# Two attentions and mixtures of experts: new instruction orders in both attentions, blocks without GpSimd's descriptor drain

## What is computed

```python
x = x + L0_xattn(_layernorm(x), ctx_1024, ctx_1024, fside, fside, pad, mask, ...)   # 16 heads of 16
x = x + L0_ffn(_layernorm(x), ...)      # 14 experts, top 2, 256 -> 512 -> 256
x = x + L1_xattn(_layernorm(x), ctx_1024, ctx_1024, mask, ...)
x = x + L1_ffn(_layernorm(x), ...)      # a shared expert, 8 experts, top 2, 256 -> 1024 -> 256
```

```python
q = (query @ Wq.T + bq).reshape(B, T, H, D).transpose(0, 2, 1, 3)
...
probs = jax.nn.softmax(scores, axis=-1)
out = jnp.einsum('bhts,bhsd->bhtd', probs, v)
```

## Time and profile before

| | us |
|---|---|
| median of 3 runs | 1040.72 (1039.98 to 1042.22) |
| profiled execution: time | 1038.13 |
| its span | 1036.3 |
| mean granted TensorE clock | 0.963 |
| PE busy | 936.5 (90%) |
| DVE, ACT, POOL busy | 498.2, 504.5, 411.6 |

### The profile page before, as it was taken

How to read it: one execution, slowest core, us unless ns; L and a number is a source line. 1 busy time by engine, 2 the same in 40 slices (tenths; PEclk the granted TensorE clock), 3 DMA queues, 4 the chain that set the end, 5 groups by cost and what they waited for, 6 DMA issues and landing times. The chain is left out here.

```text
span 1036.3 us, 25281 instructions
## 1 busy us (share of the span) xinstructions
PE 936.5 (90%) x7420; PEld 826.3 (80%) x7421; DVE 498.2 (48%) x2085; ACT 504.5 (49%) x1434; POOL 411.6 (40%) x534
## 2 busy tenths in 40 slices
PE   2799999788999999649999889998999999999992
PEld 2677787577899999536777679998999999999992
DVE  3587777564333343249999662222232323232315
ACT  2577777423333333238989743343343434343442
POOL 2777767200455555244555250000323333232213
PEclk9899999989899999859999989999999999999996
DMA  5966564077122222135221079200111111101107
GB/s 180 278 189 193 166 194 144 22 264 275 55 68 71 71 71 71 41 103 157 78 80 48 31 244 378 75 11 11 36 35 35 36 35 35 35 35 35 35 17 248
DMA packets 101321, 108.53 MB, mean 105 GB/s; under 512 B 9064, under 2 KB 87546, under 8 KB 100986
## 3 DMA queue, kind: packets, MB, share of 16 engines
q1 hardware_dynamic: 92272, 85.15, 25.6%
q0 software_dynamic: 8064, 22.03, 6.6%
q10 hardware_dynamic: 906, 0.37, 0.2%
HBM read 86.02 MB, written 21.50 MB: 104 GB/s over the span
## 5 line engine op out<-in xcount | busy, mean ns | idle before, releaser
L1846 PEld LDWEIGHTS experts_bank<-xT,wp 128*128 128x128 f32 x1968 | 234.8, 194 | 8.4 <-issue 4.4
L1846 PE MATMUL experts_bank<-xT,wp 128*128 128x128 f32 x1968 | 235.6, 277 | 3.7 <-DVE wp L1926 3.7
L1897 ACT ACTIVATE Hn<-experts_bank,vecT 128x128 f32<-128x128 f32 x312 | 114.3, 367 | 166.2 <-PE experts_bank L1846 147.4
L1778 POOL DMA_INDIRECT token_outputs<-yb,dst x84 | 94.7, 1127 | 215.6 <-DVE yb L1938 215.6
L1457 POOL DMA_INDIRECT rows<-token_rows,src x84 | 90.2, 1074 | 218.9 <-DVE dst L1452 119.6
L1856 PE MATMUL experts_bank<-w,Hn 128*128 x624 | 142.8, 382 | 0.0
L1938 DVE TENSOR_TENSOR yb<-experts_bank,b 128x256 f32<-128x256 f32 x84 | 35.7, 425 | 210.9 <-PE experts_bank L1856 210.9
L1926 DVE COPY wp<-w 128x1024 f32 x123 | 87.8, 714 | 94.7 <-PE experts_bank L1846 93.8
L1856 PEld LDWEIGHTS experts_bank<-w,Hn 128*128 128x128 f32 x624 | 115.4, 190 | 16.0
L1897 ACT ACTIVATE hid<-experts_bank,vecT 128x128 f32<-128x128 f32 x180 | 65.3, 367 | 103.1 <-PE experts_bank L1856 71.4
L1856 PE MATMUL experts_bank<-w,hid 128*128 x360 | 85.0, 379 | 0.0
(11 more groups left out here) (266 smaller groups left out, 1481.5 us busy)
## 6 DMA issues: line engine op xcount, KB each, us to landing
fs<-in_fside_Bx16xSxS_dram SPq DMA_DIRECT2D x32, 512.0 KB, 4.2
w<-in_L_ffn_w_dram SPq DMA_DIRECT2D x28, 512.0 KB
w<-in_L_ffn_Wfc_dram SPq DMA_DIRECT2D x8, 1024.0 KB, 13.8
w<-in_L_ffn_Wproj_dram SPq DMA_DIRECT2D x8, 1024.0 KB, 12.6
ctx<-in_ctx_dram SPq DMA_DIRECT2D x32, 128.0 KB, 4.8
token_rows<-Hn SPq DMA_DIRECT2D x32, 128.0 KB, 3.0
keys_values<-WT SPq DMA_DIRECT2D x16, 256.0 KB, 3.7
y<-token_outputs SPq DMA_DIRECT2D x16, 256.0 KB, 3.1
```

The lines of the kernel that those rows point to most:

```text
L1778: pool.indirect_dma_start(out=c["yg"], out_offset=bass.IndirectOffsetOnAxis(ap=routing["dst"][:, n:n + 1].bitcast(U32), axis=0), in_=yb[n ...
L1846: last = pe.matmul(HB[f % 4][:, 0:P], piece[:, i, (f % CF) * P:(f % CF + 1) * P], xT[par][:, i], start=(i == 0), stop=(i == DC - 1))
L1897: act.activation(hid[par][:, f], HB[f % 4][:, 0:P], moe.act, bias=bias).then_inc(hid_ready, 1)
```

## The change

Three edits. First, in all seven phases `nc.Block()` becomes `nc.Block(no_gpsimd_drain=True)`. In the instruction streams POOL's DRAIN ahead of the first barrier of each block's end is gone; the drains of the other engines, the DRAIN of L67 that comes with the clearing of semaphores, and that of L69 stay. Second, the order in which attention 0's engines call their functions: on PE the groups of outputs stand in two pairs instead of four single groups, project_v goes right behind project_k, and bring comes ahead of turn_e(b-1, 2); ACT has h_out ahead of q_out; DVE has stats ahead of k_out and one group of minima later; POOL has layer_norm of an element one iteration earlier and at the end. Third, the order in attention 1: on PE all four groups of outputs stand together; exps, h_out, minima, residual, et_out and stats move on ACT and DVE; POOL's layer_norm and DVE's stats take element b-1 where they took b-2, and residual and stats stand in one iteration. SP's programs are not touched. The waits of the functions stay, but for two that go from the second group of outputs to the first, since that comes first now. Of the seven hunks of the first edit one stands below.

```diff
--- before.py
+++ after.py
@@ -328,7 +328,7 @@
         ve_ready, rs_ready, nm_ready, h_ready = sem("ve_ready"), sem("rs_ready"), sem("nm_ready"), sem("h_ready")
         hT_done, hT_ready = sem("hT_done"), sem("hT_ready")
         lg_done, lg_ready = sem("lg_done"), sem("lg_ready")
-        block = stack.enter_context(nc.Block())
+        block = stack.enter_context(nc.Block(no_gpsimd_drain=True))
 
         def has(t):
             return 0 <= t < B
@@ -400,15 +400,16 @@
             normed(2)
             pool.wait_ge(amb_ready, 1)
             for b in range(-1, B + 3):
+                if has(b + 1):
+                    add_bo(b + 1)
                 if has(b):
                     bias(b, 1)
-                if has(b - 3):
-                    layer_norm(b - 3)
                 if b >= 0 and has(b + 3):
                     normed(b + 3)
                 if has(b + 1):
                     bias(b + 1, 0)
-                    add_bo(b + 1)
+                if has(b - 2):
+                    layer_norm(b - 2)
 
         @block.tensor
         def _(pe):
@@ -481,7 +482,7 @@
                 last.then_inc(et_done[g], 1)
 
             def outputs(b, g):
-                if g == 1:
+                if g == 0:
                     pe.wait_ge(v_ready, b + 1)
                     if b >= 1:
                         pe.wait_ge(on_ready, b)
@@ -537,34 +538,32 @@
             for b in range(-1, B + 3):
                 if has(b):
                     scores(b)
-                if has(b - 1):
-                    turn_e(b - 1, 2)
                 if has(b + 1):
                     bring(b + 1)
                 if has(b - 1):
-                    outputs(b - 1, 1)
+                    turn_e(b - 1, 2)
                 if has(b - 2):
                     turn_out(b - 2)
                 if has(b - 1):
                     outputs(b - 1, 0)
+                    outputs(b - 1, 1)
                     turn_e(b - 1, 3)
-                    outputs(b - 1, 2)
+                if has(b - 2):
+                    project_out(b - 2)
                 if has(b + 1):
                     project_q(b + 1)
-                if has(b - 2):
-                    project_out(b - 2)
+                if has(b - 1):
+                    outputs(b - 1, 2)
+                    outputs(b - 1, 3)
                 if has(b):
                     turn_e(b, 0)
-                if has(b - 1):
-                    outputs(b - 1, 3)
                 if has(b - 3):
                     turn_h(b - 3)
                 if has(b + 1):
                     project_k(b + 1)
+                    project_v(b + 1)
                 if has(b):
                     turn_e(b, 1)
-                if has(b + 1):
-                    project_v(b + 1)
                 if has(b - 1):
                     turn_back(b - 1)
                 if has(b - 3):
@@ -612,6 +611,7 @@
 
             for b in range(-1, B + 3):
                 if has(b - 1):
+                    exps(b - 1, 3)
                     et_out(b - 1, 2)
                 if has(b + 1):
                     in_out(b + 1)
@@ -619,14 +619,13 @@
                     exps(b, 0)
                     exps(b, 1)
                     et_out(b, 0)
+                if has(b - 3):
+                    h_out(b - 3)
                 if has(b + 1):
                     q_out(b + 1)
-                if has(b - 3):
-                    h_out(b - 3)
                 if has(b):
                     exps(b, 2)
                     et_out(b, 1)
-                    exps(b, 3)
 
         @block.vector
         def _(dve):
@@ -717,16 +716,14 @@
             mask()
             dve.wait_ge(vones_ready, 2)
             for b in range(-1, B + 3):
-                if has(b):
-                    minima(b, 3)
                 if has(b - 2):
                     residual(b - 2)
                 if has(b - 1):
                     o_out(b - 1)
+                if has(b - 2):
+                    stats(b - 2)
                 if has(b + 1):
                     k_out(b + 1)
-                if has(b - 2):
-                    stats(b - 2)
                 if has(b - 1):
                     divide(b - 1)
                 if has(b - 3):
@@ -734,13 +731,15 @@
                 if has(b + 1):
                     v_out(b + 1)
                     minima(b + 1, 0)
-                    minima(b + 1, 1)
                 if has(b - 1):
                     turned(b - 1)
+                if has(b + 1):
+                    minima(b + 1, 1)
                 if has(b):
                     et_out(b)
                 if has(b + 1):
                     minima(b + 1, 2)
+                    minima(b + 1, 3)
 
 
 def attention1(nc, sem, alloc, a, c, routing, shared, moe):
@@ -886,13 +885,13 @@
                 pool.memset(kside[i][:], 0.0).then_inc(kzero_ready, 1)
             for i in two:
                 pool.memset(vaug[i][:], 1.0).then_inc(vones_ready, 1)
-            for b in range(-3, B + 2):
-                if has(b - 2):
-                    layer_norm(b - 2)
+            for b in range(-3, B + 1):
                 if has(b + 2):
                     normed(b + 2)
                 if has(b + 3):
                     add_moe(b + 3)
+                if has(b - 1):
+                    layer_norm(b - 1)
                 if has(b + 1):
                     v_in(b + 1)
 
@@ -998,25 +997,23 @@
                     scores(b)
                 if has(b - 2):
                     turn_out(b - 2)
+                if has(b - 3):
+                    turn_h(b - 3)
                 if has(b - 1):
                     turn_e(b - 1, 2)
-                    outputs(b - 1, 1)
-                    outputs(b - 1, 0)
-                if has(b - 3):
-                    turn_h(b - 3)
                 if has(b - 2):
                     project_out(b - 2)
+                if has(b - 1):
+                    turn_e(b - 1, 3)
                 if has(b + 1):
                     bring(b + 1)
                 if has(b - 1):
-                    turn_e(b - 1, 3)
-                    outputs(b - 1, 2)
+                    for g in groups:
+                        outputs(b - 1, g)
+                if has(b):
+                    turn_e(b, 0)
                 if has(b - 3):
                     logits(b - 3)
-                if has(b - 1):
-                    outputs(b - 1, 3)
-                if has(b):
-                    turn_e(b, 0)
                 if has(b + 1):
                     project_q(b + 1)
                 if has(b):
@@ -1070,7 +1067,6 @@
 
             for b in range(-1, B + 3):
                 if has(b - 1):
-                    exps(b - 1, 1)
                     et_out(b - 1, 0)
                     exps(b - 1, 2)
                 if has(b):
@@ -1080,12 +1076,13 @@
                     exps(b - 1, 3)
                 if has(b - 2):
                     turned(b - 2)
+                if has(b - 3):
+                    h_out(b - 3)
                 if has(b - 1):
                     et_out(b - 1, 2)
-                if has(b - 3):
-                    h_out(b - 3)
                 if has(b):
                     exps(b, 0)
+                    exps(b, 1)
                 if has(b + 1):
                     in_out(b + 1)
 
@@ -1160,17 +1157,13 @@
 
             for b in range(-3, B + 3):
                 if has(b - 1):
-                    et_out(b - 1)
-                if has(b + 3):
-                    combine(b + 3)
-                if has(b - 2):
-                    stats(b - 2)
-                if has(b - 1):
                     o_out(b - 1)
                 if has(b - 3):
                     logits_out(b - 3)
                 if has(b):
                     minima(b, 3)
+                if has(b + 3):
+                    combine(b + 3)
                 if has(b - 1):
                     divide(b - 1)
                 if has(b + 2):
@@ -1178,9 +1171,14 @@
                 if has(b + 1):
                     minima(b + 1, 0)
                     minima(b + 1, 1)
-                    minima(b + 1, 2)
                 if has(b - 1):
                     residual(b - 1)
+                if has(b):
+                    et_out(b)
+                if has(b - 1):
+                    stats(b - 1)
+                if has(b + 1):
+                    minima(b + 1, 2)
 
 
 def at(b):
...
```

## The result

The changed kernel takes 1014.25 us (median of 4 runs, 1013.62 to 1015.99) against 1040.35 (4 runs, 1039.82 to 1042.22): a ratio of 0.9749, 95% interval 0.9731 to 0.9766, 26.1 us less. Forecast were 1015.5, so 25.3 less than the median before the change. The profiled execution took 1014.64, with a span of 1012.9.

A forecast was written before the change was run, and what follows sets the result against it. PE was taken to bound attention 0, three engines nearly level in attention 1, and POOL's drain to idle all engines after experts0. -7.8 - 7.2 - 7.2 - 3.1 = -25.3 from 1040.7 gives 1015.5 us, range 1011.5 to 1030.5.

The forecast's parts named there:

- The sum over islands: Attention 0 on PE: fewer separate runs of narrow output matmuls save 0.61 us an element, giving 9.62; whole term -7.8 us.
- the fourth turn_e: Attention 0 on PE: tightest operand, needing ACT's ET copy of the third; about even, charged 0.04 us an element.
- Attention 1: One run of output matmuls brings PE from 8.10 to about 7.5 us; DVE then sets the period, 7.85; -7.2 us.
- DVE with the least idle time: Sign for attention 1: DVE idles least, with scores 7.8 to 7.9 us apart and no wait for qT.
- tight place: Attention 1: xn for bring(b+1), made by POOL from DVE's statistics, is asked for earlier by PE, with all outputs queued behind.
- The drain: End of layer 0's experts: without POOL's drain the 7.25 us with every engine idle goes; -7.2 us.
- rival A: Blocks' ends: the drain's work moves to L67's DRAIN, which would take 4 to 7 us; 1029.0 us, chance 0.20.
- A2: Blocks' ends: the idle 7.2 us would hit any next POOL instruction, and the end gains nothing; 1025.7 us, chance 0.06.
- POOL's first work within 1.5 us: Sign behind layer 0's last scatter: POOL works again within 1.5 us, with no stretch of all engines idle.
- The end: Kernel's end: without POOL's drain only what lies after SP's own drain is saved, 3.0 us, with semaphore hops -3.1.
- Rival C: Attentions: waits replace the savings, attention 1 stays at 8.37 us, attention 0 gets half; 1026.5 us, chance 0.04.
- Rival D: Attention 1: PE idles more and TensorE's clock falls, +5.6 us an element, 1106 us with all 16; chance 0.03.

The follow-up runs named there:

- e6: Changed kernel with attention 0's two pairs of output groups split again into four single groups on PE, other orders kept; 1022.4 us.
- e2: Kernel before with only the change's attention 0, all engines' orders, and every block with its drain; 1030.87 us.
- e9: Changed kernel with the second of DVE's two combine operations in attention 1 done by POOL as a product and a sum; 1011.9 us.
- e8b: Changed kernel with attention 1's outputs in two pairs on PE, one ahead of bring and one behind, project_out and turn_e left in place; 1011.46 us.
- e8: Changed kernel with attention 1's outputs in two pairs on PE, the first moved ahead of project_out; 1024.0 us.
- e5: Kernel before with every second scatter of layer 0's experts issued twice, the second after the first has landed; 1075.97 us in one run.
- e4: Changed kernel with POOL's drain left out only at the end of layer 0's experts and back in the six other blocks; 1015.49 us.
- e1: Kernel before with no_gpsimd_drain=True in all seven blocks and nothing else changed; 1030.32 us.

## Why the prediction was right

*The number.* 1015.5 were forecast and 1014.25 measured, and part of this nearness is luck. In the two traces the change takes off 23.4 us, 1.9 less than the sum: the end gave 2.2 less than forecast and setup took 1.1 more, and the other phases gave 1.3 more. From median to median it is 26.1, 0.8 more than the sum. The 2.7 us between the two come from where the profiled executions lie among the runs of their kernels. Three mechanisms of four held in size; the fourth held too, but something else took most of it away.

*Attention 0.* The sum over islands holds: 9.62 by the rows, 9.63 measured, 0.59 less an element where 0.57 was charged; of the waits there is one, 0.05 at the fourth turn_e, where the prediction had it. e6 shows the cause. The phase gained 8.4 in the trace of the change and 7.7 in e2.

*Attention 1.* Forecast 7.85 with DVE as the bound, measured 7.78 with DVE 98% busy; the records of DVE overlap a little (those of L1113 are 0.29 long and stand 0.21 apart), which the prediction had as its upper bound (7.75). The phase gained 7.5 (forecast 7.2). The mechanism is the forecast one: PE comes down until DVE sets the period. PE's share was overpriced, though: its stream without waits is 7.60 (e9), 0.50 below 8.10 where 0.59 was charged, so PE had 0.19 to spare. The sign "DVE with the least idle time" fails by the row of busy time, where PE has less; it holds by the starts, where PE waits 0.19 for xn. That is the tight place the prediction had named. Merging beyond two islands hardly counts (e8b); what counts is that the orders keep DVE fed, as e8 shows by breaking that. Which of the new orders on DVE, ACT and POOL did this was not tried one by one.

*The drain.* The 7.25 us of idle are gone, and rival A, that they would turn up at L67, has fallen (59 to 145 ns). So has A2, that the idle would be there for any next instruction. The picture in A, that the length goes with the indirect DMAs, is right by e5 (0.082 us each), but not as work that must be done at the next drain: neither L67's (59 to 145 ns in the change) nor the next block's (687 ns in e4, 682 before) does it. That the work is removed and not moved was the author's estimate; no trace shows what the drain is for, only that it took 9.1 us in e5 when all 111 indirect DMAs had landed, and that nothing took its place. The sign "POOL's first work within 1.5 us" was missed (2.25): 9.55 less 7.25 would have given 2.3.

The other drains, in the trace of the kernel before: each of the seven blocks ends with a DRAIN on every one of the five engines and then an EVENT_SEMAPHORE on each, all within 0.2 us of one another (442.2 to 442.3 behind experts0); behind that stand POOL's DRAIN and EVENT_SEMAPHORE_RANGE_CLEAR of L67 (the latter 88 to 373 ns), and a DRAIN and an EVENT_SEMAPHORE on every engine at L69. The drains of L69 take 14 ns on ACT, 13 on PE, 7 on SP, 19 on DVE (136 once) and 34 to 45 on POOL. At the blocks' own ends SP's take 7 to 123; at L1722 ACT's take 379 and 934 ns, DVE's 429 and 526, PE's 2798 and 4075, POOL's 7247 and 7037.

*The end.* This is the term that was off in the change's profile: -0.9 instead of -3.1. The 3.1 were right; what failed is the step before it, that the other blocks' ends cost and gain "nothing". With the flag in most of them PE gets into experts1 0.4 us later, and the granted clock fell there in seven traces of eight; together 2.0 us.

*Rival C* has fallen: the period of attention 1 is 7.78 and not 8.37, and attention 0 gained all that was priced. *Rival D*, the clock falling in attention 1, did not come: 1.00 from 500 to 545.88 us, with PE busy for 99.6% of it. The lower level that D reckons with is 0.50: the kernel before has it in 205:207 and 435:440 of the earlier trace rows, and from 209.11 to 209.80, where the two transposes of the earlier trace rows take 0.69 us; in the two attentions it had 1.00. Such a fall came at another place, at a block's start rather than in a steady period.

*Open.* Why DVE's copy of wp and POOL's second gather in experts1 both come 0.35 us later in seven of the eight kernels with the flag in six or seven blocks, and not in the eighth, e9. And whether the longer waits bring the fall or only go with it: it fell in seven of these eight traces, in e9 with only the first wait 0.06 longer, and not in e8b, which had both. In e1, e8 and e9 the fall began 0.5 to 1.2 us into the second wait, when all that differed from the five traces without a fall was the 0.06 of the first; the length of the second wait can't have brought it there. Neither was settled.

## What to carry to other kernels

Before pricing a new order, find out for each stage which engine is never idle: in attention 0 it was PE, and each island of narrow matmuls counted (0.27 us, e6); in attention 1 PE and DVE are 0.2 us apart (7.60 in e9, 7.78 in the change), so less work on PE counted only down to DVE's time, and less on DVE only down to PE's. Look for stretches in which no engine is busy; here a block that ended behind 88 indirect DMAs of GpSimd held one of 7.25 us, and behind 111, all landed, the drain took 9.13 us (e5). When such a gap is closed, read the start of the next phases too: here 0.06 to 0.4 us of extra idle on PE went with 3.4 to 6.8 us at a granted clock of 0.50.

## What the runs showed of the hardware that I had not expected

- GpSimd's drain at a block's end cost 0.082 to 0.083 us for each indirect DMA of the block, though all had landed: 7.25 us for 88, 9.13 for 111, 6.29 for 76, 0.07 for none. Left out, it is made up for nowhere: the drain of L67 behind the block takes 0.06 to 0.15 us (change, e1, e4), and the next block's own drain ends 0.07 us behind POOL's last operation (e4).
- The granted clock of TensorE fell from 1.00 to 0.50 for 3.4 to 6.8 us at the start of a block in seven of eight traces in which PE's waits there were 1.37 and 2.06 us or one of them, and in none of six with 1.31 and 1.71.
- Narrow f32 matmuls (32 output rows) between 128-row ones cost about 0.22 (e8b against e9), 0.27 (e6) to 0.30 us (the change against the kernel before in attention 0) an island beside their own time.
